# Moving the copies of a turned adjacency from VectorE to ScalarE, and one reordering in the prologue

## The chip, the cores and the metric

The kernel runs on one core of a Trainium2 chip. The metric is the device time of one execution in microseconds, as the median of several runs. A core has TensorE (PE, matrix products into PSUM), VectorE (DVE), ScalarE (ACT), GpSimd (POOL) and SyncE (SP), which issues the DMAs. Each engine has its own list of instructions, works through it in order, and waits for others by semaphores.

## The reference, cut to what matters

Sixteen graphs of 512 nodes and 128 channels, each with a 512 x 512 adjacency, pass through four blocks, each added to x:

```python
x = x + relu(norm_adj @ (layernorm(x) @ W0.T + b0))          # norm_adj = d^-1/2 * adj * d^-1/2, d = row sums
x = x + (layernorm(x) @ Wf.T + bf)
x = x + L1_gnn(layernorm(x), adj, ...)                       # below
x = x + scan30(layernorm(x))                                 # 30 x: tanh step, silu, layernorm, matmul
```

The third block computes a 1x1 convolution, a 17-tap convolution over the nodes, an edge matrix `A = exp(-dist) * adj` from a 3-column embedding, messages `x_nmp = A @ relu(x @ w_msg.T + b_msg)`, and a GRU cell whose gates take x_conv, x_nmp and x (`gi = [x_conv, x_nmp] @ w_ih.T`, `gh = x @ w_hh.T`).

## The kernel before, in words

The first 570 us are the graph stage, the rest are the 30 iterations of the last block. The graph stage is a software pipeline over graphs. `steps` (L339) calls each engine's `step(b, p, c, d)`: graph b is in the third block, c = b + 1 in the first two, and the adjacency of d = b + 2 is turned. There are two steps for the prologue (b is None), 14 with all three graphs (b = 0 to 13), then three that drain. Nothing schedules this at run time; the order of each engine's work is that of its `step`, written out by hand.

An adjacency is turned in four pieces mt = 0 to 3 of 512 x 128 (`adj_turn`, L628; PE instructions of L634). Pieces 0 and 2 go to PSUM bank TURN_A, pieces 1 and 3 to TURN_B. Before it turns piece 2 (3) PE waits until piece 0 (1) has been copied out of its bank. `adjt_even` (L880, instruction L884, ScalarE) copies pieces 0 and 2 to `adj_t`, `adjt_odd` (L1170, instruction L1173, VectorE) pieces 1 and 3.

PE's order in a steady step, from where the turn begins: turn pieces 0 and 1; turn x for the norm of c (`turn(1, c)`, L614, waits for VectorE's norm L1166); the last distances (L685); tokens (L620); the last convolution tap; the message product (L767); turn pieces 2 and 3; then `product`s of three matmuls each (L603, L604, L605): x times w_hh for r, for z, and, once `s_adjt_odd` says that bank TURN_B is empty, for n; then the products of x_conv, the turn of x for the third block, the products of x_nmp. The next step starts with conv1, message tokens (L620), the aggregate (L625) and the embedding product.

ScalarE's order in the same stretch: exp L889 (edges), copy of piece 0, x_conv L988 and a second relu L990 (both wait for conv_pre), x_nmp L995, copy of piece 2, gh_n L1002 (waits for the third product), xc L1010 and its high half L1011, the gates. After the embedding product come four emb_f L943 and n_act L949.

VectorE's order: degree L1149 with its two small ones, h_odd, messages, gates, upd (L1271 and on), conv_pre L1288, the aggregate's scaling L1295 and sum L1297, statistics L1141, the embedding's low halves L1306, norm 1 (L1166), edges 1 and 3 (L1177), norm 3, x_tok L1332 and statistics, conv_pre L1339, copy of piece 1, copy of piece 3, norm 2, statistics 0, the low half of x_nmp L1360, of xc L1366, norm 0, then xs L1235. GpSimd makes each norm's `rstd` (L464, L466) from the statistics.

In the prologue's second step VectorE does xs of graph 0, `fold` (weights), then degree and statistics of graph 1, which wait for its DMA, and then the scaling of graph 0's aggregate. Around it stand the splitting of weights (`weights_low` L1095) and, at the end, `sums_low`, `split_bias` and xs of graph 1. The stretches of the chip's time are named by us from the span's start.

Of the kernel before, what the change touches and what calls it, by code (L numbers as in the profile page):

```python
# [23 lines left out]
ACT = mybir.ActivationFunctionType  # L24
# [56 lines left out]
def build(nc, x, adj, w0, b0, wf, bf, w_se, b_se, conv1_w, bn1, conv2_w, bn2, w_msg, b_msg,  # L81
          w_ih, b_ih, w_hh, b_hh, ln_w, ln_b, w1, b1, out):
    with ExitStack() as ctx:
# [105 lines left out]
        bank = [psum[:, i, :] for i in range(8)]  # L189
# [240 lines left out]
        @block.gpsimd  # L430
        def _(pool):

            pool.wait_ge(s_const, 1)
            pool.affine_select(out=ident[:], in_=ident[:], compare_op=ALU.is_equal, fill=0.0, base=0,
                               pattern=[[-1, P]], channel_multiplier=1).then_inc(s_ident, 1)

            def vectors():

                def pair(c):
                    return bcol[:, c:c + 2]  # L440

                count = [0]

                def link(ins):
                    count[0] += 1
                    ins.then_inc(s_chain, 1)
                    pool.wait_ge(s_chain, count[0])

                pool.wait_ge(s_small, 16 * NSMALL)
                link(pool.tensor_scalar(pair(T0), pair(V1), 1.0, EPS, ALU.mult, ALU.add))  # L450
                link(pool.tensor_tensor(pair(S0), pair(T0), half_neg[:, 0:2], ALU.pow))
                link(pool.tensor_tensor(pair(SC1), pair(S0), pair(G1), ALU.mult))
                link(pool.tensor_tensor(pair(U0), pair(M1), pair(SC1), ALU.mult))
                pool.tensor_tensor(pair(SH1), pair(BE1), pair(U0), ALU.subtract)

                link(pool.tensor_tensor(pair(S0), pair(BR), pair(HR), ALU.add))
                pool.tensor_scalar(pair(RZB), pair(S0), 0.5, None, ALU.mult)
                pool.tensor_scalar(bcol[:, HNB:HNB + 1], bcol[:, HN:HN + 1], 0.5, None, ALU.mult).then_inc(s_vectors, 1)

            def rstd(w, n):  # L460

                pool.wait_ge(s_stat[w], n + 1)
                settle(pool, s_passed_pool)
                pool.tensor_scalar(ln_ve[:, w, :], ln_stat[:, w, :, 2], 1.0 / C, EPS, ALU.mult, ALU.add).then_inc(s_rs[w], 1)  # L464
                pool.wait_ge(s_rs[w], 2 * n + 1)
                pool.tensor_tensor(ln_rs[:, w, :], ln_ve[:, w, :], half_neg[:, 0:NT], ALU.pow).then_inc(s_rs[w], 1)  # L466

            def edges(b, p, mt):
                pool.wait_ge(s_exp, 4 * b + mt + 1)
                pool.tensor_tensor(edge[:, mt, :], edge[:, mt, :], adj_t[p][:, mt, :], ALU.mult).then_inc(s_edge_p, 1)  # L470

            def slot(it, k):
                before = earlier(it, k, LAG_P)
                if before is None:
                    return
                i, j, s = before
                pool.wait_ge(f_v, s + 1)
                wait(pool, f_norm_act, act_norms(i, j + 1) - sum(ACT_TILES) // 2)
                pool.tensor_tensor(f_rs[:, j % 4, :], f_var[:, j % 2, :], half_neg[:, 0:GT], ALU.pow).then_inc(f_pow, 1)  # L479
                pool.wait_ge(f_pow, s + 1)  # L480
                wait(pool, f_turn, s - 3)
                t = GT - ACT_TILES[j] - DVE_TILES[j]
                pool.tensor_tensor(tiles(h_ring[j % 4])[:, 0:t, :], tiles(g_ring[j])[:, 0:t, :],  # L483
                                   spread(f_rs[:, j % 4, 0:t], t, C), ALU.mult).then_inc(f_norm, 1)

            def step(b, p, c, d):
                l1 = exists(b)
                if l1:

                    pool.wait_ge(s_h1, 2 * b + 1)  # L490
                    if c is not None:
                        pool.wait_ge(s_xs, c + 1)
                    inner = slice(EDGE, EDGE + INNER)
                    odd = phases(h_full[:])[:, 1, inner]
                    for k in range(2):
                        even = phases(h_full[:, 2 * k:2 * k + 2 * (EDGE + INNER)])[:, 0, inner]
                        ins = pool.tensor_tensor(diff[:, k, inner], even, odd, ALU.subtract)
                    ins.then_inc(s_diff, 1)
                    pool.wait_ge(s_diff_hi, b + 1)
                    pool.tensor_tensor(diff_s[1][:, :, inner], diff[:, :, inner], diff_s[0][:, :, inner].bitcast(F32),  # L500
                                       ALU.subtract).then_inc(s_diff_lo, 1)
                    for w in range(2):
                        pool.wait_ge(s_emb_sg, 2 * b + w + 1)
                        pool.tensor_tensor(emb_f[w][0][:], emb_f[w][0][:], emb_f[w][1][:], ALU.mult).then_inc(s_emb_v, 1)

                if b is None and c is not None:
                    pool.wait_ge(s_wload, 16 * NWEIGHTS)
                    for k in range(SUM_FILLS):
                        even, odd = (conv2_nat[:, :, 8 * k + h:8 * k + h + 7:2].rearrange("p i t -> p t i") for h in range(2))
                        pool.tensor_tensor(sum_nat[k], even, odd, ALU.add).then_inc(s_sums, 1)  # L510
                if b is None:
                    rstd(0, d)
                if c is not None:
                    rstd(1, c)
                if b is None and c is not None:
                    vectors()
                if l1:
                    edges(b, p, 0)
                if ends(b, B):
                    slot(0, 4)  # L520
                if later(b):
                    rstd(3, b - 1)
                if ends(b, B):
                    slot(0, 5)
                if l1:
                    edges(b, p, 2)
                if c is not None:
                    rstd(2, c)
                if l1:

                    pool.wait_ge(s_x_conv, 2 * b + 2)
                    wait(pool, s_z_ps, b)
                    pool.tensor_tensor(x_conv[1][:], conv_pre[:], x_conv[0][:].bitcast(F32), ALU.subtract).then_inc(s_x_conv_lo, 1)
                if d is not None:
                    if b is not None:
                        rstd(0, d)

                    pool.wait_ge(s_deg, 3 * d + 3)
                    wait(pool, s_x1, d)
                    pool.tensor_tensor(deg0[:, 2, :], deg0[:, 1, :], half_neg[:, 0:NT], ALU.pow).then_inc(s_dinv, 1)  # L540
                    pool.wait_ge(s_dinv, 2 * d + 1)
                    pool.tensor_tensor(dinv[:], deg0[:, 2, :], deg0[:, 0, :], ALU.mult).then_inc(s_dinv, 1)

            steps(pool, step)
            slots(pool, slot)

# [302 lines left out]
        def _(act):  # L849
# [30 lines left out]
            def adjt_even(c, q, mt):  # L880
# [2 lines left out]
                wait(act, s_edge_v, 2 * (c - 1))  # L883
                act.activation(adj_t[q][:, mt, :], bank[TURN_A], ACT.Copy).then_inc(s_adjt_even, 1)  # L884

            def exp(b, mt):
                act.wait_ge(s_dist, 4 * b + mt + 1)
                wait(act, s_nmp, b)
                act.activation(edge[:, mt, :], bank[DIST_A + mt % 2], ACT.Exp).then_inc(s_exp, 1)  # L889
# [34 lines left out]
            def step(b, p, c, d):  # L924
# [57 lines left out]
                    slot(0, 1)  # L982
                if d is not None:
                    adjt_even(d, p, 0)
                if l1:
                    act.wait_ge(s_conv_pre, b + 1)
                    wait(act, s_z_ps, b)
# [7 lines left out]
                    act.activation(x_nmp[0][:], bank[CHAN], ACT.Copy).then_inc(s_x_nmp, 1)  # L995
                if d is not None:
                    adjt_even(d, p, 2)
                if l1:

                    act.wait_ge(s_ghn_ps, b + 1)  # L1000
# [27 lines left out]
        def _(dve):  # L1028
# [138 lines left out]
                                            ln_rs[:, w, t:t + 1], ALU.subtract, ALU.mult)  # L1167
                ins.then_inc(s_norm[w], 1)

            def adjt_odd(c, q, mt):  # L1170
                dve.wait_ge(s_adj_turned, 4 * c + mt + 1)
                wait(dve, s_edge_p, 2 * (c - 1))
                dve.tensor_copy(adj_t[q][:, mt, :], bank[TURN_B]).then_inc(s_adjt_odd, 1)  # L1173

            def edges(b, p, mt):
                dve.wait_ge(s_exp, 4 * b + mt + 1)
# [49 lines left out]
            def step(b, p, c, d):  # L1226
# [3 lines left out]
                if l0:  # L1230
# [5 lines left out]
                                             op0=ALU.add, op1=ALU.mult).then_inc(s_xs, 1)  # L1236
                    if b is None:
                        fold()
                        degree(d, p)
                        stats(0, d)  # L1240
                if d is not None and (b is not None or not l0):
                    degree(d, p)
                    if b is None:
# [48 lines left out]
                if l0:  # L1292
# [5 lines left out]
                                             op0=ALU.max, op1=ALU.add).then_inc(s_x1, 1)  # L1298
                    dve.wait_ge(s_x1, c + 1)
                    stats(1, c)  # L1300
                if l1:

                    dve.wait_ge(s_emb_hi, 2 * b + 2)
# [37 lines left out]
                                             op1=ALU.add).then_inc(s_conv_pre, 1)  # L1341
                if ends(b, B - 1):
                    slot(0, 2)
                if d is not None:
                    adjt_odd(d, p, 1)
                if l0 and b is None:
                    weights_low(4, 6)
                    norm(2, c)
                    weights_low(6, 7)
                if d is not None:  # L1350
                    adjt_odd(d, p, 3)
                if l0 and b is not None:
                    norm(2, c)
                if d is not None and b is not None:
# [52 lines left out]
```

## Time and profile before

| | |
|---|---|
| median of 3 runs | 1344.01 us (1343.89 to 1344.42) |
| the profiled execution, whole | 1345.95 us |
| its span, first to last instruction | 1344.0 us |
| busy: PE, DVE, ACT, POOL | 94%, 90%, 75%, 71% of the span |
| mean granted PE clock | 0.983 of full speed |
| one steady step of the graph stage | 33.5 us |
| ACT copy from PSUM, 128 x 512 fp32 (L884, x32) | 597 ns median |
| DVE copy from PSUM, 128 x 512 fp32 (L1173, x32) | 688 ns median |

A row of the timeline gives an instruction's start and duration, the engine, the line of the kernel, the operation, output and input, and, in brackets, how long the engine had been idle before it and who released it. "x4" means four instructions merged into one row, with the duration of all four. The duration of a PE matmul overlaps the next one's.

### The profile page before, as it was taken

What the parts mean: (1) busy time and instruction counts of PE and PEld (TensorE: products, weight loads), DVE (VectorE), ACT (ScalarE), POOL (GpSimd) and SP (SyncE); (2) the same over time, 40 slices, a digit from 0 to 9 for tenths busy, and PEclk for the clock granted to TensorE, in tenths of its full rate; (3) what the DMA queues carried; (4) which work ended last, traced back from release to release, by engine and by line L of the source; (5) the groups of instructions that cost most, each with busy time, mean ns of one, the idle gap of its engine ahead of it and who ended that gap; (6) DMA issues with size and microseconds to landing.
All of it is one profiled execution on the core that took longest, in us unless ns stands there. A gap on an engine that the chain in (4) does not pass through costs nothing.

```text
span 1344.0 us, 29373 instructions
## 1 busy us (share of the span) xinstructions
PE 1261.2 (94%) x9227; PEld 1118.1 (83%) x9227; DVE 1215.8 (90%) x2807; ACT 1003.7 (75%) x1408; POOL 959.1 (71%) x783
## 2 busy tenths in 40 slices
PE   4799999999999999849999999999999999999998
PEld 3677777777777777639999999999999999999998
DVE  7688888888888887589999999999999999999997
ACT  1354444444444444568999999999999999999995
POOL 3244444444444444349999999999999999999996
PEclk8899999999999999979999999999999999999999
DMA  5111111111111100000000000000000000000004
GB/s 184 40 40 40 40 39 39 40 39 39 39 39 39 39 0 1 0 0 1 0 0 0 0 0 0 0 0 0 0 0 0 0 0 0 0 0 0 0 0 126
DMA packets 29792, 27.71 MB, mean 21 GB/s; under 512 B 3269, under 2 KB 21448, under 8 KB 29640
## 3 DMA queue, kind: packets, MB, share of 16 engines
q1 hardware_dynamic: 29768, 27.41, 6.4%
q8 instruction: 13, 0.21, 0.1%
q14 instruction: 11, 0.09, 0.0%
HBM read 23.21 MB, written 4.19 MB: 20 GB/s over the span
## 4 chain that ended last, share of the span: by engine, by line
PE 74%; DVE 15%; issue 5%; ACT 3%; SPq 1%; POOL 1%; DMA 0%; DVEq 0%; ACTq 0%; POOLq 0%
PE psum L825 32%; PE psum L839 16%; PE psum L821 7%; PE psum L603 4%; PE psum L605 4%; PE psum L604 4%; PE psum L625 3%; DVE xh_mem L1166 2%; PE psum L620 2%; DVE emb_n L1306 1%; DVE y_all L1166 1%; ACT emb_f L943 1%; DVE ln_stat L1141 1%; PE psum L614 1%; DVE upd L1271 1%
## 5 line engine op out<-in xcount | busy, mean ns | idle before, releaser
L897 ACT ACTIVATE g_ring<-u_ring 128x1024 f32<-128x1024 f32 x240 | 428.2, 1784 | 2.0 <-DVE u_ring L1215 2.0
L921 ACT ACTIVATE y_all<-psum 128x1024 f32<-128x1024 f32 x240 | 418.7, 1745 | 7.1 <-PE psum L839 7.1
L479 POOL TENSOR_TENSOR f_rs<-f_var,half_neg 128x8 f32<-128x8 f32 x240 | 394.3, 1643 | 29.1 <-DVE f_var L1224 9.3
L906 ACT ACTIVATE t_ring<-psum 128x1024 f32<-128x1024 f32 x232 | 409.1, 1763 | 3.4 <-PE psum L825 3.4
L825 PEld LDWEIGHTS psum<-w_t,y_all 128*128 128x128 f32 x2880 | 382.8, 193 | 9.4
L825 PE MATMUL psum<-w_t,y_all 128*128 128x128 f32 x2880 | 388.6, 275 | 0.0
L1199 DVE BATCH_NORM_STATS2 f_stat<-g_ring 128x6 f32<-128x256 f32 x960 | 341.9, 418 | 4.8 <-ACT g_ring L897 4.8
L483 POOL TENSOR_TENSOR h_ring<-g_ring,f_rs 128x640 f32<-128x640 f32 x240 | 303.2, 1263 | 18.8
L1215 DVE SCALAR_TENSOR_TENSOR u_ring<-t_ring,psum 128x1024 f32<-128x1024 f32 x232 | 278.8, 1202 | 0.0
L914 ACT ACTIVATE h_ring<-g_ring,f_rs 128x128 f32<-128x128 f32 x240 | 269.8, 1124 | 4.3 <-POOL f_rs L479 4.3
L839 PE MATMUL psum<-ident,h_ring 128*128 128x128 f32 (+1 forms) x1920 | 252.2, 275 | 7.1 <-DVE h_ring L1186 7.1
L839 PEld LDWEIGHTS psum<-ident,h_ring 128*128 128x128 f32 (+1 forms) x1920 | 232.2, 155 | 7.8 <-issue 7.8
L821 PE MATMUL psum<-bias,ones_bf 65*128 65x512 bf16 x480 | 159.6, 332 | 0.9 <-DVE u_ring L1215 0.9
L464 POOL TENSOR_SCALAR ln_ve<-ln_stat 128x4 f32<-128x4 f32 x64 | 18.5, 289 | 193.3 <-DVE ln_stat L1141 193.3
L825 PE MATMUL psum<-w1c_t,y_all 128*128 128x128 f32 x960 | 146.8, 276 | 0.0
L1186 DVE TENSOR_SCALAR h_ring<-g_ring,f_stat,f_rs 128x128 f32<-128x128 f32 x480 | 145.3, 344 | 0.2 <-POOL f_rs L479 0.2
L825 PEld LDWEIGHTS psum<-w1c_t,y_all 128*128 128x128 f32 x960 | 126.9, 193 | 0.0
L889 ACT ACTIVATE work<-psum 128x512 f32<-128x512 f32 x64 | 34.8, 595 | 101.8 <-PE psum L685 101.7
L603 PE MATMUL psum<-diff_s_h,wt_h 128*128 128x256 f32 x272 | 81.6, 300 | 0.0
L1166 DVE TENSOR_SCALAR xh_mem<-x_tok,ln_stat,ln_rs 128x128 f32 (+1 forms) x192 | 77.0, 464 | 2.6 <-POOL ln_rs L466 2.6
L604 PE MATMUL psum<-diff_s_l,wt_h 128*128 128x256 f32 x272 | 76.6, 281 | 0.0
L605 PE MATMUL psum<-diff_s_h,wt_l 128*128 128x256 f32 x272 | 76.4, 281 | 0.0
(190 smaller groups left out, 2151.5 us busy)
## 6 DMA issues: line engine op xcount, KB each, us to landing
work<-in_adj_dram SPq DMA_DIRECT2D x16, 1024.0 KB, 5.5
x_tok<-in_x_dram SPq DMA_DIRECT2D x16, 256.0 KB, 5.7
out_dram<-y_all SPq DMA_DIRECT2D x8, 512.0 KB, 3.3
work<-in_L_gnn_conv_w_dram SPq DMA_DIRECT2D x1, 1088.0 KB
work<-in_L_gnn_w_ih_dram SPq DMA_DIRECT2D x1, 384.0 KB
work<-in_L_gnn_w_hh_dram SPq DMA_DIRECT2D x1, 192.0 KB
work<-in_L_gnn_W_dram SPq DMA_DIRECT2D x1, 64.0 KB, 5.2
work<-in_L_ffn_weight_dram SPq DMA_DIRECT2D x1, 64.0 KB, 4.9
```

Source lines behind the costliest of these rows:

```text
L479: pool.tensor_tensor(f_rs[:, j % 4, :], f_var[:, j % 2, :], half_neg[:, 0:GT], ALU.pow).then_inc(f_pow, 1)
L483: pool.tensor_tensor(tiles(h_ring[j % 4])[:, 0:t, :], tiles(g_ring[j])[:, 0:t, :], spread(f_rs[:, j % 4, 0:t], t, C), ALU.mult).then_inc(f ...
L821: pe.matmul(y_ps[k % 2][:, h, 0:C * biased], ones_bf[:], bias1[:, 0:biased, :].rearrange("p t c -> p (t c)"), start=True, stop=False, skip ...
L825: m = pe.matmul(y_ps[k % 2][:, h, C * t:C * t + C], y_all[:, GT * k + NT * h + t, :], w1_t[:] if t < biased else w1c_t[:], start=False, st ...
L839: m = pe.transpose(g_ps[j % 2][0:rows, t // NT, P * (t % NT):P * (t % NT) + P], tiles(h_ring[j % 4])[:, t, 0:rows], ident[:])
L897: act.activation(g_ring[j], u_ring[j % 2], ACT.Silu).then_inc(f_silu, 1)
L906: act.activation(t_ring[k % 2], src, ACT.Tanh).then_inc(f_tanh, 1)
L914: ins = act.activation(tiles(h_ring[j % 4])[:, t, :], tiles(g_ring[j])[:, t, :], ACT.Copy, scale=f_rs[:, j % 4, t:t + 1])
L921: act.activation(y_all[:, GT * j:GT * j + GT, :].rearrange("p t c -> p (t c)"), g_ps[j % 2].rearrange("p h n -> p (h n)"), ACT.Copy).then_ ...
L1186: ins = dve.tensor_scalar(tiles(h_ring[j % 4])[:, t, :], tiles(g_ring[j])[:, t, :], f_stat[:, j % 4, 0, t, 1:2], f_rs[:, j % 4, t:t + 1], ...
L1199: ins = dve.bn_stats(f_stat[:, j % 4, 0, 2 * q:2 * q + 2, :].rearrange("p t w -> p (t w)"), both)
L1215: dve.scalar_tensor_tensor(out=u_ring[k % 2], in0=t_ring[k % 2], scalar=STEP, in1=src, op0=ALU.mult, op1=ALU.add).then_inc(f_u, 1)
```

## The change

ScalarE gets a function `adjt_odd` beside `adjt_even` and copies all four pieces: 0 and 1 together where it copied 0, 2 and 3 together where it copied 2. VectorE's `adjt_odd` and its two calls are gone. The new copy also waits for VectorE's edge products of the graph before. In the prologue, VectorE's degree and statistics of graph 1 move from behind `fold` to behind the first graph's aggregate and its statistics, and GpSimd's `rstd(1, c)` moves ahead of `rstd(0, d)`, in the prologue (where b is not None `rstd(0, d)` stands elsewhere).

```diff
@@ GpSimd, step
+                if c is not None:
+                    rstd(1, c)
                 if b is None:
                     rstd(0, d)
-                if c is not None:
-                    rstd(1, c)
@@ ScalarE
+            def adjt_odd(c, q, mt):
+                act.wait_ge(s_adj_turned, 4 * c + mt + 1)
+                wait(act, s_edge_p, 2 * (c - 1))
+                wait(act, s_edge_v, 2 * (c - 1))
+                act.activation(adj_t[q][:, mt, :], bank[TURN_B], ACT.Copy).then_inc(s_adjt_odd, 1)
+
...
                 if d is not None:
                     adjt_even(d, p, 0)
+                    adjt_odd(d, p, 1)
...
                 if d is not None:
                     adjt_even(d, p, 2)
+                    adjt_odd(d, p, 3)
@@ VectorE
-            def adjt_odd(c, q, mt):
-                dve.wait_ge(s_adj_turned, 4 * c + mt + 1)
-                wait(dve, s_edge_p, 2 * (c - 1))
-                dve.tensor_copy(adj_t[q][:, mt, :], bank[TURN_B]).then_inc(s_adjt_odd, 1)
...
                     if b is None:
                         fold()
-                        degree(d, p)
-                        stats(0, d)
...
                     dve.wait_ge(s_x1, c + 1)
                     stats(1, c)
+                    if b is None:
+                        degree(d, p)
+                        stats(0, d)
...
                 if ends(b, B - 1):
                     slot(0, 2)
-                if d is not None:
-                    adjt_odd(d, p, 1)
                 if l0 and b is None:
                     weights_low(4, 6)
                     norm(2, c)
                     weights_low(6, 7)
-                if d is not None:
-                    adjt_odd(d, p, 3)
                 if l0 and b is not None:
                     norm(2, c)
```

## Rows read from the trace of the kernel before

**Rows 1.** The page, part 1: busy us, share of the span, instructions.

```profile
PE 1261.2 (94%) x9227; PEld 1118.1 (83%) x9227; DVE 1215.8 (90%) x2807; ACT 1003.7 (75%) x1408; POOL 959.1 (71%) x783
```

**Rows 2.** Waits of PE, 60 to 540 us: total us, times, longest us.

```profile
PE psum L614 <- DVE xh_mem L1166: 17.1, 14, 2.0
PE psum L634 <- DVE work L1173: 15.1, 13, 1.2
```

**Rows 3.** Timeline, the start of a steady step: PE, ScalarE, VectorE (start us, us).

```profile
254.23 0.40 PE L605 MATMUL psum<-xc_s_h,wse_l 128*105 128x512 f32 x1
...
254.66 2.79 ACT L943 ACTIVATE emb_f<-psum,emb_vec 105x512 f32<-105x512 f32 x4 [0.52 <-PE psum L605]
...
258.09 1.27 DVE L1271 TENSOR_TENSOR upd<-xc,n_act 128x512 f32<-128x512 f32 x1 [1.31 <-ACT n_act L949]
```

**Rows 4.** Timeline of VectorE in the same step, from conv_pre on.

```profile
275.28 0.73 DVE L1339 SCALAR_TENSOR_TENSOR conv_pre<-psum,bcol,conv_pre 128x512 f32<-128x512 f32 x1
275.93 0.68 DVE L1173 COPY work<-psum 128x512 f32<-128x512 f32 x1
...
277.97 1.78 DVE L1166 TENSOR_SCALAR xh_mem<-x_tok,ln_stat,ln_rs 128x128 f32 x4
```

**Rows 5.** Timeline of PE, the same step: turns of pieces 2 and 3, third product.

```profile
274.90 0.60 PE L634 MATMUL psum<-ident,work 128*128 128x128 f32 x4
276.67 0.66 PE L634 MATMUL psum<-ident,work 128*128 128x128 f32 x4 [1.17 <-DVE work L1173]
...
278.56 0.39 PE L603 MATMUL psum<-xc_s_h,wt_h 128*128 128x512 f32 x1
...
279.02 0.39 PE L605 MATMUL psum<-xc_s_h,wt_l 128*128 128x512 f32 x1
```

**Rows 6.** Timeline of ScalarE, the same step: pieces 0 and 2, x_conv, x_nmp.

```profile
273.03 0.60 ACT L884 ACTIVATE work<-psum 128x512 f32<-128x512 f32 x1 [1.88 <-POOL work L470]
276.05 0.72 ACT L988 ACTIVATE x_conv_h<-conv_pre,bcol 128x512 fp32r<-128x512 f32 x1 [2.42 <-DVE conv_pre L1339]
...
277.43 0.58 ACT L995 ACTIVATE x_nmp_h<-psum 128x512 fp32r<-128x512 f32 x1
277.91 0.59 ACT L884 ACTIVATE work<-psum 128x512 f32<-128x512 f32 x1
```

**Rows 7.** Timeline of the prologue: VectorE's low half of xc, PE's product behind it.

```profile
43.49 0.69 DVE L1366 TENSOR_TENSOR xc_s_l<-xc,xc_s_h 128x512 fp32r<-128x512 f32 x1 [0.70 <-ACT xc_s_h L1011]
...
44.33 0.47 PE L603 MATMUL psum<-xc_s_h,wt_h 128*128 128x512 f32 x1 [0.92 <-DVE xc_s_l L1366]
...
44.87 0.39 PE L605 MATMUL psum<-xc_s_h,wt_l 128*128 128x512 f32 x1
```

**Rows 8.** Timeline of VectorE in the prologue.

```profile
23.70 2.29 DVE L1149 TENSOR_REDUCE deg<-work 128x4 f32<-128x2048 f32 x1 [2.39 <-DMA x_tok<-in_x_dram]
...
26.85 0.67 DVE L1295 TENSOR_TENSOR agg_tok<-psum,dinv 128x512 f32<-128x512 f32 x1
...
28.39 0.77 DVE L1141 BATCH_NORM_STATS2 ln_stat<-x_tok 128x6 f32<-128x256 f32 x2
30.67 1.11 DVE L1166 TENSOR_SCALAR xh_mem<-x_tok,ln_stat,ln_rs 128x128 f32<-128x128 f32 x4 [1.52 <-POOL ln_rs L466]
...
38.72 0.69 DVE L1173 COPY work<-psum 128x512 f32<-128x512 f32 x1 [1.82 <-PE psum L634]
...
50.10 0.69 DVE L1235 SCALAR_TENSOR_TENSOR xs<-xh_mem,dinv 128x512 f32<-128x512 f32 x1
```

**Rows 9.** Timeline of PE in the prologue: the first graph's aggregate becomes tokens.

```profile
24.67 1.13 PE L620 MATMUL psum<-w_full,xh_t 128*128 128x128 f32 x8 [0.78 <-ACT xh_t L953]
```

**Rows 10.** Windows: start:end, length, busy of each engine (instructions), PEclk, DMA share, GB/s.

```profile
40.00:45.00 5.00, 2.51 (x17) 1.90 (x16) 4.30 (x14) 2.37 (x5) 0.00 (x0) 1.00 0.57 214
534.00:538.00 4.00, 1.97 (x15) 1.56 (x14) 3.97 (x9) 1.45 (x3) 1.62 (x2) 1.00 0.00 0
538.00:542.00 4.00, 4.00 (x15) 3.08 (x14) 2.76 (x7) 1.32 (x3) 2.78 (x3) 0.57 0.00 0
```

## The prediction

> **What bounds the kernel now.** I read the page first. TensorE (PE) is busy for 94% of the span [rows 1], but the change touches only the graph stage, so that stage has to be read alone. There, who waited for whom on PE, from 60 to 540 us, gives just two waits that repeat: PE waits for VectorE's norm before the turn of x (14 times, 17.1 us) and for VectorE's copy of a turned adjacency (13 times, 15.1 us) [rows 2]. Those are all of PE's waits in 480 us. So a step of the pipeline is a closed loop, and I follow it round once, in the step from 254 us on. The loop has three legs.
>
> Leg one: PE ends the embedding product at 254.63; ScalarE starts its four emb_f activations at 254.66, then n_act, and VectorE, which sat idle for 1.31 us, starts upd at 258.09 [rows 3]. Leg two: VectorE works down its own list to conv_pre (275.28, ends 276.01) and then copies turned piece 1 out of PSUM (275.93, ends 276.61) [rows 4]. Leg three: PE, idle for 1.17 us, starts the turn of piece 3 at 276.67 [rows 5] and from there runs without a wait until the next embedding product. A step later the same legs come again, 33.5 us apart. Whoever makes PE's third leg later makes every step longer by as much.
>
> **The steady steps, part by part.** The edit is live in the steps that turn another adjacency beside a running graph: 14 of them (b = 0 to 13); two in the prologue are treated below.
>
> *Taken away:* VectorE's copy of piece 1 no longer stands between conv_pre and PE's piece 3. ScalarE makes it instead, right behind its copy of piece 0, which starts at 273.03 [rows 6]; it would end by about 274.2. Nothing is queued behind it: ScalarE's next work, x_conv, waits for conv_pre until 276.05, idle for 2.42 us [rows 6]. PE ends its turn of piece 2 at 275.50 and can start piece 3 at once, 1.2 us earlier than now. The 1.17 us wait is gone. That is worth 13 x 1.17 = 15.2 us, if nothing is late next.
>
> *What is late next:* piece 3's copy. PE's third product behind the turns (h times w_hh, third part, into the bank TURN_B) must wait until that copy has emptied the bank. Today VectorE makes it beside ScalarE's work and PE doesn't wait: the product's first matmul starts at 278.56, its last ends at 279.02 + 0.39 = 279.41 [rows 5]. In the changed kernel the copy is the fifth in ScalarE's list after conv_pre: x_conv (276.05), a second relu, x_nmp (277.43), copy of piece 2 (277.91), copy of piece 3 [rows 6]. All of these stand back to back already, and the first can't start before VectorE's conv_pre ends at 276.01 [rows 4], which the change doesn't touch: it lies ahead of the removed copy. Copies follow each other at 277.91 - 277.43 = 0.48 to 0.50 us, so piece 3's starts at 278.41 and ends 0.59 later, at 279.00.
>
> PE restarts 0.06 us behind a releaser (276.61 to 276.67 [rows 4, 5]), or 0.15 (VectorE's end at 43.49 + 0.69 = 44.18 to PE's 44.33 [rows 7]). A product of this kind that starts from a stop takes from 44.33 to 44.87 + 0.39 = 45.26, 0.93 us [rows 7]. So it ends at 279.00 + (0.06 to 0.15) + 0.93 = 279.99 to 280.08, where it now ends at 279.41: **0.58 to 0.67 us later per step**, I take 0.62. PE, ready for it at 278.56 - 1.17 = 277.4, waits until 279.06 to 279.15, about 1.7 us, in place of 1.17 there. Behind it stand gh_n's release, the products of x_conv and all the rest of leg three, which has no slack. 14 x 0.62 = 8.7 us longer; by the bounds 8.1 to 9.4, and if a copy's step or the restart is off by 0.1 us, 6.7 to 10.8.
>
> *On VectorE* two copies of 0.68 leave. Behind conv_pre comes the norm of x for the next graph, 277.97 now [rows 4]; it may start an us earlier. Its readers on PE come behind the third product, so nothing is gained by that, and VectorE's start in the next step is set by n_act [rows 3]. I count nothing.
>
> A rule speaks against this change. The Trainium skill, "ScalarE: Activation LUTs", section "Rules for kernel authors", gives relu, max, min, add and mul to VectorE rather than ScalarE, and a plain copy is nearest to these. Here the rows differ with it: from PSUM in fp32 ScalarE takes 0.59 us [rows 6] and VectorE 0.68 [rows 4]. Were ScalarE's copy no faster than VectorE's, the step would grow by about 0.1 us more, 1.4 in all.
>
> **The prologue.** The DMA of the second graph holds VectorE's degree until 23.70 us; degree and its statistics take until the aggregate's scaling starts at 26.85, so 3.15 us [rows 8]. PE has the tokens ready at 24.67 + 1.13 = 25.80 [rows 9]. Changed, the scaling starts at about 25.86, statistics 1 start 1.54 us later (26.85 to 28.39 [rows 8]) and take about 0.67 (0.77 less the overlap with the next), so degree starts at 28.07 and its block ends at 31.22. Only then comes the norm which now starts at 30.67 [rows 8]: 0.55 us *later*, since that norm used to wait for GpSimd and the block was free in the DMA's shadow. On GpSimd the order of the two rstd goes with it; with rstd 1 still behind rstd 0, it would wait for statistics that come last.
>
> Further down, VectorE waits for PE before it copies piece 1, which starts at 38.72 [rows 8], and splits weights and norms behind it. At most that gives back its idle 1.82 and two copies. But each stage of what follows is moved by 0.55, and PE and ScalarE get in the way. My working for them: PE turns piece 3 behind ScalarE's copy of piece 1, at about 40.05, and turns x at 40.5 to 41.15; ScalarE, with one more copy ahead, reaches xc at 41.25, and VectorE its low half two copies later, at 42.36, now 43.49 [rows 7]. From there VectorE is busy without a gap until xs at 50.10 [rows 8], for which PE sits idle. So the prologue ends **1.1 us earlier**. PE, idle before, may get its full clock back a stretch sooner or later: a stretch at 1.2 GHz as from 538 us on [rows 10] costs about half its length, 1.7 us, so the bounds are 2.8 us earlier and 0.6 later.
>
> **Sum.** 8.7 - 1.1 = +7.6 us on a profiled span of 1344.0. The profiled execution is 1345.95, 1.9 around the span; the median of the runs is 1344.01, so I put the difference on the median: **1351.6 us**. Its own range, from 6.7 - 2.8 to 10.8 + 0.6, is 1347.9 to 1355.4.
>
> **Rivals.**
>
> *A, nothing is late next (faster).* If piece 3's copy came out of ScalarE before PE wants the bank at 277.4, the whole wait would go: 1344.0 - 15.2 - 1.1 = 1327.7. It speaks for this that ScalarE is idle 2.42 us before x_conv [rows 6]; against it that this idle time lies before conv_pre and the copy must stand behind it. The point from which it decides: the copy would have to end 0.62 us earlier than I say for the change merely to break even, 1.7 earlier for all of it. A milder form is that VectorE is the true bound and its 1.36 us per step count: 14 x (0.62 - 1.36) - 1.1 = -11.5, 1332.5. VectorE's idle 1.31 us before upd [rows 3] speaks against it. Together 9%.
>
> *B, the delay is absorbed (same).* Leg three would need slack behind the third product, and PE shows none [rows 2]. Then only the prologue counts: 1342.9, up to 1346. 8%.
>
> *C, the clock falls (slower still).* The granted clock stood at 2.4 GHz from 40 to 45 us, where PE was busy for 2.51 of 5 us, and from 534 to 538, with 1.97 of 4 busy, it stood as well, but right after that, from 538 on, it went to 1.2 GHz for most of 4 us [rows 10]. PE's stop there is 2.0 us, the longest of the 14 [rows 2]. A stop of 1.7 lies between it and today's 1.17. Each fall would cost about half of such a stretch, 1.7 us, on leg three. With 2 to 7 falls, 3.4 to 12 us, at 4 falls 1358.4. 13%.
>
> *The forecast* keeps 70%.
>
> **Range and chances.** The range runs from 1346.0 to 1358.0: it takes in the forecast, some of B, and more than half of C, and leaves out A. About 0.2%, 2.7 us, is what a measurement of this kernel can tell from no change, so same is 1341.3 to 1346.7. Faster 0.09 (A), same 0.08 (B), slower 0.83 (forecast and C).
>
> **What would show it.** Right: no wait of PE on a copy before the turn of piece 3; in its place one of about 1.7 us, 14 times (0.4 us in step 0), before the first matmul of the third product, released by ScalarE's copy; steps of 34.1 us in place of 33.5; PE's wait for the norm unchanged at 1.2; xs of the second graph at about 49.0. Wrong: conv_pre sooner after the embedding product than 21.4 us, the third product starting before piece 3's copy has ended, or a clock under 2.4 GHz inside the steady steps.

## The result, and the profile after

The changed kernel takes **1350.45 us** (median; 1348.94 to 1351.42), the kernel before, run beside it, 1344.42 (1343.89 to 1345.98). The ratio is 1.0042, with a 95% interval of 1.0027 to 1.0056: slower by 6.0 us. The profiled execution took 1351.42 us, with a span of 1349.5, 5.5 more than before. Forecast were 1351.6 and +7.6.

The page, part 1 (busy us, share of the span, instructions), to be read against [rows 1], and a line of part 4 (the chain that ended last, by engine):

```profile
PE 1259.8 (93%) x9227; PEld 1117.1 (83%) x9227; DVE 1198.6 (89%) x2775; ACT 1019.1 (76%) x1440; POOL 960.4 (71%) x783
PE 73%; DVE 14%; ACT 5%; issue 5%; POOL 1%; DVEq 0%; DMA 0%; ACTq 0%; SPq 0%; POOLq 0%
```

VectorE lost 32 instructions and 17.2 us of work, ScalarE gained 32 and 15.4 us, PE still carries 73% of the chain, and the kernel is slower. Busy time says nothing here; the waits do. Waits of PE, changed kernel, 60 to 545 us (total us, times, longest us), against [rows 2]:

```profile
PE psum L603 <- ACT work L890: 22.4, 14, 1.7
PE psum L614 <- DVE xh_mem L1174: 17.0, 14, 2.0
```

The 15.1 us for VectorE's copy are gone, and 22.4 for ScalarE's copy of piece 3 (L890) stand in their place. The norm's line is what it was. The rise in waiting is 22.4 - 15.1 = 7.3 us; the 13 steps between the second and the 15th of the 16 embedding products grew by less. The last matmul of that product starts at 86.61 and 522.52 us before, at 87.03 and 528.02 after, so a step takes 33.92 us in place of 33.53. That is **0.39 per step, 5.1 us in 13**, with 0.4 more ahead of the second.

The changed kernel's timeline of the steady step that answers to [rows 4 to 6] (start us, us), ScalarE first, then PE:

```profile
275.38 0.60 ACT L884 ACTIVATE work<-psum 128x512 f32<-128x512 f32 x1 [1.88 <-POOL work L470]
275.87 0.59 ACT L890 ACTIVATE work<-psum 128x512 f32<-128x512 f32 x1
278.40 0.72 ACT L995 ACTIVATE x_conv_h<-conv_pre,bcol 128x512 fp32r<-128x512 f32 x1 [1.94 <-DVE conv_pre L1344]
279.15 0.72 ACT L997 ACTIVATE conv_pre<-conv_pre,bcol 128x512 f32<-128x512 f32 x1
279.78 0.58 ACT L1002 ACTIVATE x_nmp_h<-psum 128x512 fp32r<-128x512 f32 x1
280.26 0.59 ACT L884 ACTIVATE work<-psum 128x512 f32<-128x512 f32 x1
280.74 0.60 ACT L890 ACTIVATE work<-psum 128x512 f32<-128x512 f32 x1
...
277.25 1.04 PE L634 MATMUL psum<-ident,work 128*128 128x128 f32 x8
...
281.39 0.50 PE L603 MATMUL psum<-xc_s_h,wt_h 128*128 128x512 f32 x1 [1.70 <-ACT work L890]
```

The turns of pieces 2 and 3 now run in one (x8), with no wait between. ScalarE copies piece 1 (275.87) in time it had idle. Behind conv_pre its five activations stand back to back, the last is piece 3's copy, it ends at 281.34, and PE starts the third product 0.05 us later, after a wait of 1.70. The step's first two legs are as before: from the embedding product to x_conv it is 276.05 - 254.23 = 21.82 us before [rows 3, 6], 278.40 - 256.59 = 21.81 after.

### The profile page after: what moved, and what is told of

It is laid out like the page before. It is cut to its first block, busy times and chain, and to the rows that moved or that the text cites. A ratio compares the mean times of both kernels' runs of the same rounds, so it can differ in the third digit from the quotient of the medians.

```text
span 1349.5 us, 29373 instructions
## 1 busy us (share of the span) xinstructions
PE 1259.8 (93%) x9227; PEld 1117.1 (83%) x9227; DVE 1198.6 (89%) x2775; ACT 1019.1 (76%) x1440; POOL 960.4 (71%) x783
## 4 chain that ended last, share of the span: by engine, by line
PE 73%; DVE 14%; ACT 5%; issue 5%; POOL 1%; DVEq 0%; DMA 0%; ACTq 0%; SPq 0%; POOLq 0%
PE psum L825 32%; PE psum L839 15%; PE psum L821 7%; PE psum L603 4%; PE psum L605 4%; PE psum L604 4%; PE psum L625 3%; DVE xh_mem L1174 2%; PE psum L620 2%; DVE emb_n L1311 1%; DVE ln_stat L1149 1%; DVE y_all L1174 1%; ACT emb_f L949 1%; PE psum L614 1%; DVE upd L1273 1%
## 5 line engine op out<-in xcount | busy, mean ns | idle before, releaser
L903 ACT ACTIVATE g_ring<-u_ring 128x1024 f32<-128x1024 f32 x240 | 319.4, 1331 | 1.1 <-DVE u_ring L1219 1.1
L927 ACT ACTIVATE y_all<-psum 128x1024 f32<-128x1024 f32 x240 | 309.0, 1287 | 7.5 <-PE psum L839 7.5
L912 ACT ACTIVATE t_ring<-psum 128x1024 f32<-128x1024 f32 x232 | 300.3, 1294 | 2.9 <-PE psum L825 2.9
L920 ACT ACTIVATE h_ring<-g_ring,f_rs 128x128 f32<-128x128 f32 x240 | 159.8, 666 | 4.3 <-POOL f_rs L479 4.3
L1174 DVE TENSOR_SCALAR xh_mem<-x_tok,ln_stat,ln_rs 128x128 f32 (+1 forms) x192 | 81.0, 485 | 14.9 <-POOL ln_rs L466 14.7
```

The costliest lines, as they stand in the source:

```text
L903: act.activation(g_ring[j], u_ring[j % 2], ACT.Silu).then_inc(f_silu, 1)
L912: act.activation(t_ring[k % 2], src, ACT.Tanh).then_inc(f_tanh, 1)
L920: ins = act.activation(tiles(h_ring[j % 4])[:, t, :], tiles(g_ring[j])[:, t, :], ACT.Copy, scale=f_rs[:, j % 4, t:t + 1])
L927: act.activation(y_all[:, GT * j:GT * j + GT, :].rearrange("p t c -> p (t c)"), g_ps[j % 2].rearrange("p h n -> p (h n)"), ACT.Copy).then_ ...
```

## The experiments

Each time is a median with its lowest and highest; a ratio is to the kernel before, run beside it on the same chip, with its 95% interval. "Step" is the mean of the 13 intervals from above (before 33.53, after 33.92).

**Each part alone.** e1_copies is the changed kernel with the prologue's order of before; e2_prologue is the kernel before with the prologue's new order.

```
e1 (from after):   pool: rstd(0, d) again ahead of rstd(1, c)
                   dve:  degree(d, p), stats(0, d) again behind fold()
e2 (from before):  pool: rstd(1, c) ahead of rstd(0, d)
                   dve:  degree(d, p), stats(0, d) behind stats(1, c)
```

> The four copies on ScalarE, the prologue as before. Theory (PE's third product waits for ScalarE's fourth copy, 0.57 us later per step than today, and 0.16 us comes back because the low half of x_nmp on VectorE is no longer late for PE): 14 waits of about 1.7 us, steps of 33.92 us against 33.54, time + 5.5 us, and the second graph's xs earlier than in the changed kernel, at about 49 us, since norm 1 isn't delayed by degree: so 1348.5 to 1350. Rival (the prologue's edit carries the loss): time within 1 us of before.

> The reordering of the prologue alone, copies as before. Theory: norm 1 starts 0.55 us later (31.2), PE restarts later and keeps 1.2 GHz for a stretch longer, so the second graph's xs comes 0.5 to 2 us later than 50.10; steps stay 33.54 us; time 1344.5 to 1346.5. Rival (it brings what the changed kernel gained): xs earlier than 50.10 and a time under 1344.

Measured: e1 1351.3 us (1349.84 to 1351.86), ratio 1.0043 (1.0029 to 1.0057), +5.8 us, span 1347.8, step 33.94. e2 1347.08 us (1346.1 to 1348.6), ratio 1.001 (1.0001 to 1.002), +1.6 us, span 1346.4, step 33.51. Both times lie above the expected ranges, e1's by 1.3 us and e2's by 0.6, but the kernel before took 1345.51 beside them, and the differences are near those expected (+5.5 for e1). The copies make the steps longer, the order of the prologue doesn't. The two timed differences add up to 7.4, where both parts together gave 6.0; the intervals allow it. How large the reordering's own share is, the times alone leave open: 1.6 by e2, 0.2 by after less e1.

In the prologue the traces tell more. VectorE's norm 1 and xs of the second graph, e1 first, then the changed kernel with its degree as well, against [rows 8]:

```profile
30.61 1.11 DVE L1174 TENSOR_SCALAR xh_mem<-x_tok,ln_stat,ln_rs 128x128 f32<-128x128 f32 x4 [1.52 <-POOL ln_rs L466]
...
48.98 0.69 DVE L1239 SCALAR_TENSOR_TENSOR xs<-xh_mem,dinv 128x512 f32<-128x512 f32 x1
```

```profile
25.89 0.69 DVE L1297 TENSOR_TENSOR agg_tok<-psum,dinv 128x512 f32<-128x512 f32 x1 [4.41 <-PE psum L620]
...
28.14 2.27 DVE L1157 TENSOR_REDUCE deg<-work 128x4 f32<-128x2048 f32 x1
...
31.26 1.10 DVE L1174 TENSOR_SCALAR xh_mem<-x_tok,ln_stat,ln_rs 128x128 f32<-128x128 f32 x4
...
50.21 0.69 DVE L1239 SCALAR_TENSOR_TENSOR xs<-xh_mem,dinv 128x512 f32<-128x512 f32 x1
```

From norm 1 to xs it takes 19.43 us before [rows 8], 18.37 in e1, 18.95 in the changed kernel. So e1's copies give back 1.06 us of the prologue. In the changed kernel's profiled execution that gain is gone again: norm 1 comes 0.59 later than before, and from there to xs it takes 0.58 more than in e1. Where that second part goes shows in the windows (start:end, length, busy of PE, PEld, DVE, ACT, POOL with instructions, PEclk, DMA share, GB/s), e1 first, then the changed kernel:

```profile
33.00:37.00 4.00, 3.42 (x16) 3.42 (x17) 2.55 (x7) 0.98 (x2) 0.11 (x1) 0.50 0.01 4
37.00:41.00 4.00, 3.68 (x29) 3.19 (x28) 3.25 (x9) 3.49 (x11) 2.42 (x4) 0.95 0.00 0
```

```profile
33.00:37.00 4.00, 3.31 (x16) 3.25 (x16) 3.00 (x7) 0.87 (x2) 2.05 (x8) 0.52 0.02 4
37.00:41.00 4.00, 3.70 (x20) 3.12 (x19) 3.44 (x10) 2.96 (x9) 2.42 (x4) 0.63 0.00 0
```

From 37 to 41 us PE runs at 2.4 GHz nearly throughout in e1 (0.95 in the column of the granted clock; 1.00 in the kernel before), but at 1.2 for most of it in the changed kernel (0.63), and gets through 20 matmuls instead of 29. In e2 that stretch stands at 0.50, and norm 1 to xs takes 53.45 - 32.79 = 20.66 us, 1.23 more than before. e2's profiled execution began some 1.5 us later than the others, so only such distances can be used of it.

The new order doesn't always bring the slow stretch. e5, described below, has the changed kernel's prologue and shows the same as it, 0.63 and 18.95 us. e6 has that prologue too, with one small copy more on ScalarE, and runs at 2.4 GHz there (VectorE, then the window):

```profile
31.05 1.10 DVE L1179 TENSOR_SCALAR xh_mem<-x_tok,ln_stat,ln_rs 128x128 f32<-128x128 f32 x4
...
48.87 0.69 DVE L1244 SCALAR_TENSOR_TENSOR xs<-xh_mem,dinv 128x512 f32<-128x512 f32 x1
```

```profile
37.00:41.00 4.00, 3.67 (x32) 3.13 (x31) 3.13 (x9) 3.75 (x12) 2.42 (x4) 1.00 0.00 0
```

From norm 1 to xs e6 takes 17.82 us, 1.13 less than the changed kernel, and its xs comes 1.23 us sooner than the kernel before's. So of what the changed kernel's profile lost in the prologue, the later norm 1 belongs to the new order: VectorE now goes from degree to norm 1 without a pause, where before it waited 1.52 us for GpSimd [rows 8]. The rest goes with the clock of the one execution. Whether the order makes a slow stretch more likely, one profile of each kernel doesn't show.

**One copy of the two.** e3_piece1 gives only piece 1 to ScalarE, e4_piece3 only piece 3; VectorE keeps the other.

```
e3 (from before):  act: adjt_even(d, p, 0)  + adjt_odd(d, p, 1)
                   dve:                     - adjt_odd(d, p, 1)
e4 (from before):  act: adjt_even(d, p, 2)  + adjt_odd(d, p, 3)
                   dve:                     - adjt_odd(d, p, 3)
```

> From the kernel before: ScalarE copies piece 1, VectorE keeps piece 3. Theory: the wait before the turn of piece 3 (13 x 1.17) goes, and no wait on ScalarE comes before the third product, since VectorE copies piece 3 right behind conv_pre. The next thing late is GpSimd's low half of x_conv, which ends 2.88 us behind conv_pre: PE waits there for about 0.9 us, and a step gets shorter by 0.2 to 0.4 us: 1338.5 to 1341.5. Rival (the copies of piece 1 and 3 don't matter, another wait of the loop binds): steps of 33.54 us or longer.

> From the kernel before: VectorE keeps piece 1, ScalarE copies piece 3. Theory: PE still waits 1.17 us before the turn of piece 3, and then about 0.5 us more before the third product; piece 3's copy ends at the same distance behind conv_pre as in the changed kernel, so the steps are as long as there, 33.9 us, and the time is 1349 to 1351: taking VectorE's copy of piece 1 away was worth nothing by itself while piece 3's is ScalarE's. Rival (both moves cost or gain on their own, and add up): steps of about 34.25 us, since the copy of piece 1 alone on ScalarE made them 0.33 shorter than before.

Measured: e3 1340.61 us (1340.15 to 1341.27), ratio 0.9964 (0.995 to 0.9978), span 1339.3, step 33.20. e4 1351.73 us (1351.22 to 1352.1), ratio 1.0049 (1.0032 to 1.0066), span 1350.1, step 33.94. Waits of PE from 60 us on, e3 and then e4:

```profile
PE psum L614 <- DVE xh_mem L1173: 17.0, 14, 2.0
PE psum L603 <- POOL x_conv_l L533: 12.8, 13, 1.0
```

```profile
PE psum L614 <- DVE xh_mem L1173: 17.1, 14, 2.0
PE psum L634 <- DVE work L1180: 15.1, 13, 1.2
PE psum L603 <- ACT work L890: 4.4, 14, 0.3
```

e4 settles what the removed wait is worth beside a late piece 3: it *keeps* the old wait of 1.2 us and its step is as long as that of the changed kernel, where the wait is gone. PE comes late to the turn and waits 0.3 behind it (I had put 0.5), or comes early and waits 1.7; the third product starts behind ScalarE's fifth activation either way. My rival for e4, that the two delays add up (a step of 34.25), is out. e3 is the other half: with piece 3 left on VectorE, a step gets 0.33 us shorter, and not 1.17. GpSimd's low half of x_conv (L533) is late next, by 0.98, so the removed wait itself brings about 0.19. The rest is a second wait that no list shows and that e3 loses too; it is the subject of "The missing 0.2 us" below.

**Sooner and later by a measured amount.** e5_ahead_nmp is the changed kernel with ScalarE's copies of pieces 2 and 3 moved ahead of x_nmp's; e6_dose is the changed kernel with an extra copy of 224 columns ahead of piece 3's.

```
e5 (from after):  act: adjt_even(2), adjt_odd(3), then x_nmp   (before: x_nmp first)
e6 (from after):  + if mt == 3:
                  +     wait(act, s_spare, c)
                  +     act.activation(spare[:], bank[TURN_B][:, 0:224], ACT.Copy).then_inc(s_spare, 1)
```

> The changed kernel with ScalarE's copies of pieces 2 and 3 ahead of its x_nmp. Theory: piece 3's copy ends 0.48 us sooner, so each step is 0.48 us shorter than in the changed kernel, 33.44 us, and the time 1350.4 - 6.7 = 1343.7. Rival (ScalarE's load as such, or the clock, makes the steps longer): steps stay at 33.9 us, time at 1350.

> The changed kernel with one small extra ScalarE copy (224 columns out of the same bank, into a spare tensor) ahead of the copy of piece 3. Rows of this case give about 0.28 us for it between neighbours. Theory (the end of piece 3's copy sets the third product and with it the step): each step longer by the whole of it, 34.20 us, PE's wait 1.7 + 0.28 = 2.0 us, time 1350.4 + 3.9 = 1354.3. Rival (the loop has slack there, the loss comes from somewhere else): steps of 33.92 us, 1350.4.

Measured: e5 1344.26 us (1343.24 to 1346.62), ratio 0.9991 (0.9982 to 1.0001), span 1342.9, step 33.46. e6 1354.86 us (1354.22 to 1357.7), ratio 1.008 (1.0063 to 1.0097), span 1352.1, step 34.31. Waits of PE, e5 and then e6, and last, from e6's timeline, its extra copy with the next:

```profile
PE psum L614 <- DVE xh_mem L1174: 17.1, 14, 2.0
PE psum L603 <- ACT work L890: 15.8, 13, 1.2
```

```profile
PE psum L605 <- ACT work L895: 26.0, 14, 2.0
PE psum L616 <- DVE xh_mem L1179: 15.0, 13, 1.2
```

```profile
280.03 0.36 ACT L894 ACTIVATE spare<-psum 128x224 bf16<-128x224 f32 x1
280.26 0.61 ACT L895 ACTIVATE work<-psum 128x512 f32<-128x512 f32 x1
```

One activation fewer ahead of piece 3's copy (0.48 us) makes the step 0.47 shorter; 0.23 us more (280.26 - 280.03) makes it 0.26 longer in 12 of 13 steps (34.18 on average). The step follows the end of that copy one to one in both directions: it is the gate. The remaining step took 35.84. Right behind its stop of 1.95 us the granted clock falls (e6, windows as above):

```profile
278.00:281.00 3.00, 1.05 (x6) 0.52 (x4) 2.48 (x6) 2.84 (x6) 1.75 (x2) 1.00 0.56 157
281.00:284.00 3.00, 3.00 (x11) 2.33 (x12) 0.85 (x2) 0.69 (x1) 2.38 (x4) 0.73 0.79 280
284.00:287.00 3.00, 3.00 (x12) 2.48 (x11) 1.10 (x3) 1.77 (x3) 0.01 (x1) 0.70 0.00 0
287.00:290.00 3.00, 3.00 (x18) 2.44 (x17) 2.97 (x5) 1.85 (x3) 0.30 (x1) 1.00 0.00 0
```

PE had been busy for 1.05 of 3 us; then it is at 1.2 GHz for more than half of six. The step is 1.66 us longer than the mean of the other 12, near the 1.7 that rival C put on a fall. The other 12 stops of e6 before that product are as long (1.93 to 1.96 us) and are followed by no fall.

**The missing 0.2 us.** The third product ends late by about the 0.58 us computed, and the step grows by 0.39. Something on leg three gives the difference back. The third product ends at 279.41 before and at 281.95 + 0.40 = 282.35 after, 25.18 and 25.76 behind the start of the embedding product's last matmul; between the turn of x (L614) and the product of x_nmp behind it the starts are closer by 0.16. The kernel before, VectorE and PE, then PE of the changed kernel:

```profile
280.36 0.66 DVE L1360 TENSOR_TENSOR x_nmp_l<-psum,x_nmp_h 128x512 fp32r<-128x512 f32 x1
...
280.66 0.60 PE L614 MATMUL psum<-ident,xh_mem 128*128 128x128 f32 x4
281.17 0.47 PE L603 MATMUL psum<-x_nmp_h,wt_h 128*128 128x512 f32 x1
```

```profile
283.58 0.60 PE L614 MATMUL psum<-ident,xh_mem 128*128 128x128 f32 x4
283.93 0.48 PE L603 MATMUL psum<-x_nmp_h,wt_h 128*128 128x512 f32 x1
```

0.51 us before, 0.35 after. VectorE's low half of x_nmp ends at 281.02, 0.15 ahead of the product: a wait that no list of waits shows, since the durations printed for the two matmuls overlap. e8_nmp_first is the kernel before with that one VectorE operation moved ahead of statistics 0.

```
e8 (from before):  dve: - stats(0, d)  ahead of x_nmp's low half
                        + stats(0, d)  behind it
```

> The kernel before, with VectorE's low half of x_nmp ahead of its statistics 0 instead of behind. Theory: in the kernel before PE's first product of x_nmp starts 0.51 us behind the turn of x where it takes 0.35 in the changed kernel, because the low half ends only at 281.02; with it 0.7 us sooner that 0.16 goes: steps of 33.38 us against 33.54, time 2.2 us less than before. Rival (0.51 is no wait, but how that product starts): steps of 33.54.

Measured: 1343.16 us (1341.56 to 1344.01), ratio 0.9984 (0.9974 to 0.9993), span 1340.7, step 33.38, 0.15 shorter. Its turn of x and x_nmp's product:

```profile
278.76 0.60 PE L614 MATMUL psum<-ident,xh_mem 128*128 128x128 f32 x4
279.12 0.48 PE L603 MATMUL psum<-x_nmp_h,wt_h 128*128 128x512 f32 x1
```

0.36 us between the starts: the hidden wait was there and cost what was read from the gap. In e3 the same two starts are 0.35 apart:

```profile
277.44 0.60 PE L614 MATMUL psum<-ident,xh_mem 128*128 128x128 f32 x4
277.79 0.48 PE L603 MATMUL psum<-x_nmp_h,wt_h 128*128 128x512 f32 x1
```

So e3's 0.33 us are 0.19 from the removed wait (1.17 - 0.98) and 0.16 from the hidden one, 0.35 by the rows.

**Better than both.** e7_stats0 is e3 with, in the prologue only, statistics 0 behind statistics 1 (the degree stays in the shadow of the DMA). e9_xconv_dve adds to e7 the step of e8 and gives the low half of x_conv, e3's late operation, from GpSimd to VectorE.

```
e7 (from e3):  pool: rstd(1, c) ahead of rstd(0, d)
               dve:  stats(0, d) behind stats(1, c), degree(d, p) where it was
e9 (from e7):  dve:  adjt_odd(3), + x_conv[1] (low half), norm(2, c),
                     x_nmp[1], stats(0, d)
               pool: - x_conv[1]
```

> As e3 (ScalarE piece 1, VectorE piece 3), with the prologue's statistics 0 behind statistics 1 and rstd 0 behind rstd 1, while degree stays in the shadow of the DMA. Theory (the changed kernel's prologue lost because degree, 2.5 us, came ahead of norm 1): norm 1 starts 0.6 us sooner than in e3, at about 30.1, the second graph's xs at 48.0 to 48.7 against 49.32, steps as in e3, 33.20 us, time 1339 to 1340.5. Rival (any reordering there delays norm 1, as rstd 1 is what it waits for): xs at 49.3 or later, 1340.6 or more.

> ScalarE copies piece 1, VectorE piece 3 (as e3), VectorE also makes the low half of x_conv (GpSimd did) behind the copy of piece 3, and that of x_nmp ahead of statistics 0; in the prologue statistics 0 stand behind statistics 1 and rstd 0 behind rstd 1. Theory: with GpSimd's 1.3 us replaced by VectorE's 0.7, the low half of x_conv ends 0.6 to 0.7 us sooner behind conv_pre than in e3, the wait of 0.9 shrinks to 0.3, and steps are 32.5 to 32.7 us: 1330 to 1334. Rival (VectorE, given more work again, is late with norm 2, or the prologue loses it): steps of 33 us or more, 1337 to 1345.

Measured: e7 1338.94 us (1336.72 to 1341.11), ratio 0.9955 (0.994 to 0.9971), span 1339.2, step 33.19; e9 **1334.35 us** (1333.08 to 1334.79), ratio 0.9922 (0.9905 to 0.9938), span 1331.0, step 32.61. e7 against e3 can't be told: 0.9955 beside 0.9964, intervals overlapping. Its xs came at 49.75, no sooner than e3's 49.32; but in its profiled execution the second graph's DMA, and with it the degree, came 1.39 us later (25.19 for 23.80), and norm 1 only 0.76 later (31.51 for 30.75). Counted from the degree, norm 1 was 0.63 sooner. The expectation (norm 1 at 30.1, xs at 48.0 to 48.7) was missed. e9 has the same order in the prologue, and its degree starts at 23.73, as early as e3's: there norm 1 starts at 30.07, 0.68 sooner than in e3, and xs at 47.77, 1.55 sooner. Part of that is the clock again (granted 1.00 from 37 to 41 us, 0.88 in e3), so only the gain at norm 1 can be put down to the order.

e9 is the best version here, with steps as expected and a time 0.35 us above the expected range. Its waits of PE, and from its timeline VectorE behind conv_pre:

```profile
PE psum L609 <- DVE xh_mem L1168: 17.1, 14, 2.0
PE psum L598 <- DVE x_conv_l L1356: 6.1, 14, 1.3
```

```profile
269.59 0.69 DVE L1356 TENSOR_TENSOR x_conv_l<-conv_pre,x_conv_h 128x512 fp32r<-128x512 f32 x1 [0.90 <-ACT conv_pre L992]
270.20 1.11 DVE L1168 TENSOR_SCALAR xh_mem<-x_tok,ln_stat,ln_rs 128x128 f32 x4
```

The wait of 1.0 in e3 for x_conv's low half is down to about 0.4. From before: 1.17 removed, 0.38 new in this step, 0.16 hidden and gone make 0.95 by the rows; the step is 0.93 shorter. e9 changes three things against e3. The time between the two, 5.5 us with each set against the kernel before beside it, is told apart only by these rows.

## Why the prediction was right

**Sign, cause and time were right**: 1350.45 in a range of 1346.0 to 1358.0, 1.2 from the number. Point by point:

- *The wait for VectorE's copy goes*: yes, [rows 2] against the list above.
- *Piece 3's copy is late next, fifth in ScalarE's list, and PE waits 1.7 us*: yes, 1.70, and 22.4 in total. e5 and e6 show that this copy is the gate, e4 that moving piece 3 alone makes the step as long, and e2 that the prologue's order leaves it as it was.
- *The third product 0.58 to 0.67 later*: 25.76 - 25.18 = 0.58. Right, at the low end: PE restarts 0.05 behind ScalarE's copy (281.34 to 281.39), as it does behind VectorE's in [rows 4, 5], and the 0.15 from [rows 7] was the wrong neighbour.
- *The step grows by as much, 0.62; 14 x 0.62 = +8.7*: **mis-sized**, 0.39; 5.4 us in 14 steps, from xs of the second graph (0.11 later) to the 15th embedding product (5.50 later). The step of the argument that failed is "leg three runs without a wait", read off the list of waits, and with it "on VectorE I count nothing". In the kernel before there was a hidden wait of 0.16 for VectorE's low half of x_nmp; two copies fewer on VectorE and a later PE do away with it. 0.58 less 0.16 is 0.42, and e8 shows the 0.16 by itself (0.15).
- *The prologue 1.1 us sooner*: **mis-sized**, 0.1 later (xs at 50.21 for 50.10). Norm 1 came at 31.26, for 31.22 forecast. The term that the rows point to is the clock's, which stood at nothing in the number and only in the bounds (2.8 earlier to 0.6 later): in this profile PE ran at 1.2 GHz for most of the stretch from 37 to 41 us, and VectorE's low half of xc started at 43.60, forecast 42.36. In e6, where the same order ran at 2.4 GHz there, it started at 42.26 and xs at 48.87, for 42.36 and 49.0 forecast. That e1's xs, 48.98, is near 49.0 as well is chance: the 49.0 stood for both parts of the change, and e1 has only the copies.
- *The sum*: +7.6, measured +5.5 in the span (5.1 in the 13 steps, 0.4 ahead of them) and +6.0 in the medians. The steps gave 3.3 less than forecast and the prologue 1.2 more, so the total is closer than its parts are, and that is luck.
- *Rival A*: out; the milder form, VectorE as the true bound, too: 17.2 us less work on it and no step shorter. *Rival B*, slack behind the third product: wrong as a whole, but a quarter of it was there, the hidden wait. *Rival C*: not in the changed kernel. Its granted clock from 100 to 500 us is 1.00, with PE stopped for 1.68 to 1.70 us in each step. In e6, at 1.95, one step of 13 shows what C described, in size too.
- *"PE's wait for the norm unchanged at 1.2"*: yes, 17.0 in total for 17.1.
- *The rule on ScalarE and simple operations* (the Trainium skill, "ScalarE: Activation LUTs", "Rules for kernel authors"): the rows don't bear it out for fp32 from PSUM. ScalarE's new copies take 0.59 and 0.60, VectorE's took 0.68. The place in the queue made this kernel slower, not the engine's speed.

## What to carry to other kernels

Ahead of moving work to a less busy engine, write down for each moved piece what stands before it in the new queue and who waits for its end: piece 1 stood behind nothing and its move gained, piece 3 stood behind four operations that wait for the same chain, and its move cost more. A wait that is removed is worth only the distance to what is late next (in e3 0.19 of 1.17 us), and that can be read off ahead of time. The list of waits can leave out a short stop, here one of 0.16 us, where the records of matmuls overlap; compare the distance between two starts with the same pair elsewhere before calling a stretch free of waits.

## What was not expected of the hardware

**VectorE beside GpSimd.** The norm of x for the next graph, four operations of 128x128, takes 2.07 us in the changed kernel, where GpSimd makes the low half of x_conv beside it, and 1.11 in e9, where GpSimd is idle. VectorE and GpSimd of the changed kernel:

```profile
279.23 2.07 DVE L1174 TENSOR_SCALAR xh_mem<-x_tok,ln_stat,ln_rs 128x128 f32 x4 [0.87 <-POOL ln_rs L466]
280.01 1.29 DVE L1174 TENSOR_SCALAR xh_mem<-x_tok,ln_stat,ln_rs 128x128 f32 x1
...
279.95 1.26 POOL L533 TENSOR_TENSOR x_conv_l<-conv_pre,x_conv_h 128x512 fp32r<-128x512 f32 x1 [0.76 <-ACT conv_pre L997]
```

0.96 us more, of the 1.26 that GpSimd works, and all of it falls on the fourth operation, the second row: it starts 0.06 us behind GpSimd's and ends at 281.30, 0.09 behind the end of GpSimd's. The Trainium skill, "SBUF — State Buffer", section "SBUF: two separate sides", has the two engines share a pair of ports as an exclusive lock, the later one standing still until the first is done, if VectorE's operation is in a two-port mode or has two inputs in SBUF. The trace agrees with a lock: the fourth operation is held to GpSimd's end, and the three that started ahead of GpSimd's aren't slowed. Which mode these operations are in, no run here shows. So the 0.69 us that e9 puts on VectorE come back there with the norm.

**The clock and the length of a stop.** 13 stops of 1.68 to 1.70 us in the changed kernel brought no fall. Of 13 stops of 1.93 to 1.96 us in e6 one did, and it cost 1.66 us. It was 1.95 long, as were five others: the length of the stop alone doesn't decide it, and what sets that one apart these runs don't show.
